# Splitting the gated rows of a hybrid transformer block: ScalarE rounds, VectorE subtracts, GpSimd leaves the chain

## The reference, cut to what matters

```
normed = _rmsnorm(x, scale2)
ffn = _silu(normed @ w_gate.T) * (normed @ w_up.T) @ w_down.T      # 256 -> 1024 -> 256
x = x + ffn
```

## Time and profile before

| | value |
|---|---|
| median of 3 runs | 1556.13 us (1555.75 to 1557.9) |
| the profiled execution | 1559.04 us, of which the profile's span is 1557.0 us |
| TensorE matmul busy | 1467.0 us, 94% of the span |
| VectorE busy | 1104.2 us, 71% |
| ScalarE busy | 664.3 us, 43% |
| GpSimd busy | 556.1 us, 36% |
| turn of the loop | 92.06 us (the same instruction of ScalarE starts at 1005.88 and at 1097.94 us) |

### The profile page before, as it was taken

How to read it: one execution, slowest core, us unless ns; L and a number is a source line. 1 busy time by engine, 2 the same in 40 slices (tenths; PEclk the granted TensorE clock), 3 DMA queues, 4 the chain that set the end, 5 groups by cost and what they waited for, 6 DMA issues and landing times.

```text
span 1557.0 us, 25479 instructions
## 1 busy us (share of the span) xinstructions
PE 1467.0 (94%) x8792; PEld 1047.6 (67%) x8840; DVE 1104.2 (71%) x2127; ACT 664.3 (43%) x971; POOL 556.1 (36%) x705
## 2 busy tenths in 40 slices
PE   8899999999997699999989899999999999999998
PEld 7444444444342478888868687878888787888787
DVE  6888888888888755555585877776867777775542
ACT  1577777777766232223334233323334333332211
POOL 6446555555450232123222322323332232331420
PEclk9899999999998799999999999999999999999999
DMA  4423323323230400101100001001010100100001
GB/s 117 110 57 76 71 56 70 74 62 67 60 73 2 139 28 28 41 28 50 41 14 28 14 1 41 1 15 27 0 40 0 28 13 1 40 0 14 14 1 27
DMA packets 56414, 61.04 MB, mean 39 GB/s; under 512 B 15733, under 2 KB 41637, under 8 KB 56349
## 3 DMA queue, kind: packets, MB, share of 16 engines
q1 hardware_dynamic: 42653, 43.89, 10.7%
q0 software_dynamic: 13408, 16.29, 4.9%
q10 hardware_dynamic: 288, 0.00, 0.0%
HBM read 25.51 MB, written 8.90 MB: 22 GB/s over the span
## 4 chain that ended last, share of the span: by engine, by line
PE 50%; issue 20%; DVE 14%; POOL 8%; ACT 4%; SPq 1%; DMA 1%; another core or an unknown queue 0%; POOLq 0%; DVEq 0%; ACTq 0%
PE ps L1963 14%; PE ps L1991 9%; PE ps L960 5%; PE ps L945 4%; PE ps L931 4%; PE ps L888 3%; POOL h L1566 3%; POOL kT L1539 2%; PE ps L1974 2%; DVE mc L632 2%; PE ps L1949 1%; PE ps L2003 1%; PE ps L898 1%; DVE race L731 1%; DVE top L730 1%
## 5 line engine op out<-in xcount | busy, mean ns | idle before, releaser
L632 DVE TENSOR_REDUCE mc<-ps 128x2 f32<-128x1024 f32 x256 | 305.4, 1220 | 47.3 <-PE ps L931 46.7
L1991 PE MATMUL ps<-w_hi,h 128*128 128x256 f32 x1024 | 220.0, 299 | 11.2 <-DVE h L1803 11.2
L1870 ACT ACTIVATE h<-ps 128x512 fp32r<-128x512 f32 x128 | 76.1, 598 | 315.1 <-PE ps L2021 198.8
L1991 PEld LDWEIGHTS ps<-w_hi,h 128*128 128x128 f32 x1024 | 166.7, 190 | 19.7 <-DVE h L1803 17.6
L346 POOL DMA_DIRECT2D k_st<-k_hi x256 | 124.2, 490 | 141.8 <-PE ps L945 75.7
L1803 DVE SCALAR_TENSOR_TENSOR h<-ps,h 128x512 fp32r<-128x512 f32 x128 | 87.8, 690 | 121.9 <-ACT h L1870 119.2
L1566 POOL TENSOR_TENSOR h<-hf,h 128x512 fp32r<-128x512 f32 x56 | 72.3, 1292 | 277.6 <-DVE h L1816 277.6
L1963 PE MATMUL ps<-xT_b,w_hi 128*128 128x512 f32 x512 | 167.5, 408 | 0.0
L1991 PE MATMUL ps<-w_lo,h 128*128 128x256 f32 x512 | 143.7, 281 | 0.0
L945 PE MATMUL ps<-q_st,k_st 64*128 64x512 f32 x512 | 122.6, 478 | 16.2 <-ACT pT1a L818 5.1
L945 PEld LDWEIGHTS ps<-q_st,k_st 64*128 64x128 f32 x512 | 48.5, 187 | 118.3 <-ACT pT1b L818 46.0
(11 more groups left out here) (276 smaller groups left out, 3439.4 us busy)
## 6 DMA issues: line engine op xcount, KB each, us to landing
q_st<-q_hi SPq DMA_DIRECT2D x256, 32.0 KB, 2.1
k_st<-k_hi POOLq DMA_DIRECT2D x256, 32.0 KB, 1.9
q_st<-q_lo SPq DMA_DIRECT2D x128, 32.0 KB, 2.0
k_st<-k_lo POOLq DMA_DIRECT2D x128, 32.0 KB, 1.9
x<-in_x_dram SPq DMA_DIRECT2D x8, 512.0 KB, 4.0
x_dram<-x SPq DMA_DIRECT2D x8, 512.0 KB, 2.9
yn<-x_dram SPq DMA_DIRECT2D x16, 256.0 KB, 3.7
x<-x_dram SPq DMA_DIRECT2D x16, 256.0 KB, 3.8
```

What stands on the lines that cost most here:

```text
L632: v.tensor_reduce(mc[par][:, qt, 2 * HU + j:MC:NPAIR], ps[:, at:at + 2, :], AX_X, ALU.max).then_inc(max_done, 1)
L1870: a.activation(h[s][m % 2][0][:, :], ps[:, RING[s] + m % 2, :], ACT.Relu).then_inc(F[s]["relu"], 1)
L1991: last = t_.matmul(ps[:, ACC[s] + t // 2, (t % 2) * D:(t % 2 + 1) * D], h[s][m % 2][a][:, t * P:(t + 1) * P], ws[k][:, m, :], start=m == 0 ...
```

## The change

The high part is now written by ScalarE (a Copy activation from `hf`), and the low part by VectorE, as the second half of its step `u`; it waits for ScalarE between its two instructions. GpSimd's function `low_h` is gone. ScalarE's `u` step is new: it waits for the product (`pd`) and, from m = 2 on, for the matmuls that read the buffer (`dm`). All three lists are written anew with the same names in another order. The core of it:

```diff
 def gated(j, m, s=1, S=G):                      # VectorE
     buf = hf[s][m % 2][:, :]
     v.tensor_tensor(buf, ps[:, RING[s] + 1, :], buf, ALU.mult).then_inc(S["pd"], 1)
-    if m >= 2:
-        eng.wait_ge(S["dm"], NM * j + m - 1)
-    elif s == 0:
-        eng.wait_ge(LS["xy"], 1)
-    eng.wait_ge(S["pd"], NM * j + m + 1)
-    v.tensor_copy(h[s][m % 2][0][:, :], buf).then_inc(S["hh"], 1)
+    eng.wait_ge(S["hh"], NM * j + m + 1)
+    hi, lo = h[s][m % 2]
+    v.tensor_tensor(lo[:, :], buf, hi[:, :].bitcast(F32), ALU.subtract).then_inc(S["hl"], 1)
-def low_h(i, s, m, S, done):                    # GpSimd
-    eng.wait_ge(S[done], NM * i + m + 1)
-    hi, lo = h[s][m % 2]
-    g.tensor_tensor(lo[:, :], hf[s][m % 2][:, :], hi[:, :].bitcast(F32), ALU.subtract).then_inc(S["hl"], 1)
+def gated_hi(j, m, s=1, S=G):                   # ScalarE, new
+    if m >= 2:
+        eng.wait_ge(S["dm"], NM * j + m - 1)
+    elif s == 0:
+        eng.wait_ge(LS["xy"], 1)
+    eng.wait_ge(S["pd"], NM * j + m + 1)
+    a.activation(h[s][m % 2][0][:, :], hf[s][m % 2][:, :], ACT.Copy).then_inc(S["hh"], 1)
```

The stretches of the lists that the prediction speaks of, before (-) and after (+):

```diff
 # START, where g first meets rec
-"g.T", "z.o5", "g.m0", "g.u0", "z.o6", "g.m1", "o.x", "g.u1", "z.o7", "z.o8", "g.d0", "g.m2", "rec0", "rec1", "g.u2",
-"rec2", "g.d1", "rec3", "rec4", "g.m3", "rec5", "rec6", "g.u3", "g.d2", "rec7", "z.y", "g.m4", "g.u4", "o.mean"
+"z.o5", "z.o6", "g.T", "z.o7", "z.o8", "g.m0", "rec0", "g.u0", "g.m1", "o.x", "rec1", "g.u1", "rec2", "g.d0", "g.m2",
+"rec3", "g.u2", "g.d1", "rec4", "g.m3", "g.u3", "g.d2", "rec5", "g.m4", "rec6", "g.u4", "g.d3", "rec7", "g.m5", "z.y",
+"g.u5", "o.mean"
 # MERGED, f1 with rec
-"rec5", "f1.m4", "rec6", "f1.d3", "o.rms", "f1.m5", "f1.d4", "f1.m6", "f1.d5", "f1.m7", "f1.d6", "f1.d7"
+"f1.m4", "f1.d3", "rec5", "f1.m5", "f1.d4", "rec6", "f1.m6", "o.rms", "f1.d5", "f1.m7", "f1.d6", "f1.d7"
 # MERGED, g
-"g.m6", "g.u6", "z.rms", "g.d5", "g.m7", "g.u7", "g.d6", "z.T", "g.d7"   # o.wo ahead of g.m6
+"g.m6", "o.wo", "g.u6", "z.rms", "g.d5", "g.m7", "g.u7", "z.T", "g.d6", "g.d7"
 # CLOSE
-"g.u3", ..., "g.m6", "g.u6", "o.T", "g.d5", "z.y", "g.m7", "o.wo", "o.x", "e.rms", "g.u7", "g.d6", "e.gT"
+"o.T", "z.y", "g.u3", "g.d2", "g.m4", "g.u4", "g.d3", "o.wo", "g.m5", "g.u5", "g.d4", "g.m6", "g.u6", "g.d5", "g.m7",
+"o.x", "e.rms", "g.u7", "e.gT"
 # CLOSE, the last names
-"f1.d6", "f0.d6", "f1.d7", "f0.d7", "f1.end", "e.end"
+"f1.d6", "f1.d7", "f1.end", "f0.d6", "f0.d7", "e.end"
```

More of the change, by code:

```diff
@@ L1153 @@
 W_STREAM.insert(W_STREAM.index("g.u1") + 1, "o.x")
-START = ["p0.mask", "p1.mask", "p0.T", "p1.T", "p0.wo", "p1.wo", "init0", "p0.x", "f0.ln", "f0.T", "f0.rt",
[31 rows of a table removed]
+START = ["p0.mask", "p1.mask", "p0.T", "p1.T", "init0", "p0.wo", "p1.wo", "p0.x", "f0.ln", "f0.T", "f0.rt",
[31 rows of a table added]
 def counted(names):
@@ L1198 @@
 BEFORE = list(counted(START))
-MERGED = ["g.T", "rec7", "g.m0", "g.u0", "o.x", "g.m1", "g.u1", "g.d0", "g.m2", "g.u2", "o.mean", "z.y", "o.ln",
[6 rows of a table removed]
-CLOSE = ["g.T", "rec7", "g.m0", "g.u0", "g.m1", "g.u1", "o.mean", "o.ln", "g.d0", "g.m2", "g.u2", "g.d1",
-         "g.m3", "g.u3", "g.d2", "g.m4", "g.u4", "g.d3", "g.m5", "g.u5", "g.d4", "g.m6", "g.u6", "o.T", "g.d5",
-         "z.y", "g.m7", "o.wo", "o.x", "e.rms", "g.u7", "g.d6", "e.gT", "e.x", "g.d7", "g.end", "e.m0", "e.u0",
[7 rows of a table removed]
+MERGED = ["g.T", "rec7", "g.m0", "g.u0", "o.x", "g.m1", "g.u1", "g.d0", "g.m2", "g.u2", "o.mean", "g.d1", "z.y",
[6 rows of a table added]
+CLOSE = ["g.T", "rec7", "g.m0", "g.u0", "g.m1", "g.u1", "o.mean", "g.d0", "o.ln", "g.m2", "g.u2", "g.d1",
[9 rows of a table added]
 Z_NEXT = Z_START[1:] + steps("z.o", NOUT) + ["og"] + steps("rec", T8)[:CUT]
@@ L1579, in pool @@
         parts["e.ln"] = lambda i: ffn_ln(FIRST, 0, last_turn(1))
-        for m in range(NM):
-            parts[f"e.u{m}"] = lambda j, m=m: low_h(0, 0, m, LS, "hh")
-        for m in range(NM):
-            parts[f"g.u{m}"] = lambda j, m=m: low_h(j, 1, m, G, "hh")
         run(eng, parts)
@@ L1936, in act @@
             parts[f"e.m{m}"] = lambda j, m=m: silu(0, m, 0, LS)
+            parts[f"g.u{m}"] = lambda j, m=m: gated_hi(j, m)
+            parts[f"e.u{m}"] = lambda j, m=m: gated_hi(0, m, 0, LS)
         parts |= {"e.gT": lambda j: high(last_turn(0), 0, s2), "e.T": lambda j: high(last_turn(1), 0)}
```

## The result

The changed kernel takes 1548.99 us, the median of 5 runs (1547.52 to 1550.66). The kernel before took 1556.28 us beside it (5 runs, 1555.75 to 1557.9). The ratio is 0.9946 with a 95% interval of 0.9936 to 0.9957: 0.5% faster, 7 to 8 us. Forecast was 1547, with 1543 to 1551 as its own range. The profiled execution took 1549.59 us (span 1547.8), 0.6 us above this median; that of before took 1559.04, 2.8 us above its own. So the two traces lie 9.2 us apart where the medians lie 7.3 apart.

What follows compares the result with a forecast made beforehand. TensorE was taken to bound the kernel, busy 1467.0 of 1557.0 us. Terms of -5.1 (closing), -3.0 (loop), 0, 0 and -0.8 (end) summed to -8.9, put on the 1556.13 median: 1547 us, range 1543 to 1551.

Steps and rivals of the forecast that it cites:

- The closing stretch: After the loop: two TensorE waits and the slow clock go (5.8 us), a later Silu costs 0.7; -5.1 us.
- the loop: Five turns, each 0.6 us shorter from the dense and routed parts together; -3.0 us in all.
- `START`: Opening list: routed steps and weight splits only shuffled with the same contents; 0 us, bounds -3 and +3.
- the tail: Kernel's end: the last `f1` block's store starts two `d` earlier and doesn't share the DMA queue; -0.8 us.
- the late Silu: Tile 3's Silu comes about 0.9 us later behind ScalarE's rounding, stalling TensorE's next gate by 0.7 us.
- The routed part of a turn: In the loop: the 0.71 us wait shrinks to 0.1, the 0.48 stays, 0.3 of small gaps go.
- The dense part of a turn: In the loop: new stalls of 0.7 and 0.3 us against gains of 0.45 and 0.2; 0.3 us slower.
- rival C: VectorE's new subtraction is held by GpSimd's `o.x` or decay steps, costing TensorE 5 us; 1552 us, chance 0.08.
- rival A: Only the closing stretch and the end gain; in the loop new stalls eat the routed part's gain; 1550 us, chance 0.20.
- Where `g` meets `rec`: First meeting, 860 to 900 us: old stalls and slow clock (9 us) replaced by equal new stalls; 0, bounds -6 and +5.
- B: VectorE becomes the bound of the dense part, each turn paying 2 us; slower, 1564 us, chance 0.15.
- D: The first meeting also loses its stalls and slow clock without new ones, -6 us more; 1541 us, chance 0.12.

Runs made afterwards that it cites:

- e3: The changed kernel with the CLOSE list of the kernel before: 1557.91 us, ratio 1.0004.
- e4: The kernel before in its old roles, with the new CLOSE list but `o.x` moved behind `rec7`: 1553.58 us, ratio 0.9978.
- e6: The changed kernel with one GpSimd wait more, so that in the loop `o.x` starts after the low part of tile 1: 1546.28 us, ratio 0.9924.
- e1: The changed kernel's new roles with all three lists of the kernel before: 1563.61 us, ratio 1.0042.
- e2: The kernel before in its old roles, with only the START list of the changed kernel: 1561.42 us, ratio 1.0033.
- e10: The roles of e9 (ScalarE rounds, GpSimd subtracts) with the lists of e8: 1555.39 us, ratio 0.9985.
- e8: The kernel before in its old roles, with the new early START, the new routed part of MERGED and the CLOSE of e4: 1548.26 us, ratio 0.9936.
- e9: e1 with the subtraction given back to GpSimd, ScalarE still rounding, lists of the kernel before: 1564.53 us, ratio 1.0043.
- e5: The changed kernel with the Silu `g.m3` moved ahead of `o.ln`, and `z.y` behind it, in MERGED: 1550.77 us, ratio 0.9949.
- e11: The changed kernel with the later `o.x` of e6 and `g.d5` moved behind `g.u7` in MERGED: 1546.12 us, ratio 0.9919.

## Why the prediction was right, and where it was not

The time was right to 2 us, the direction too. The closing stretch, on which most of the sum rested, went as reasoned. That the rest fits too is partly luck: the loop gave 2.5 us less than its term, and `START`, put at nothing, gave about as much. By its steps:

**The closing stretch: right.** Predicted -5.1, measured -5.2 from the first gate to the last matmul. For the tail predicted -0.8, measured -0.6: the four transfers took 3.3 us to land, 3.8 in the earlier trace rows. GpSimd in the closing stretch of after: the addition near its head, then nothing for 21.69 us, until ScalarE's squares call for the root:
```profile
1414.82 2.40 POOL L1555 TENSOR_TENSOR x<-x,y 128x1024 f32<-128x1024 f32 x1 [15.09 <-DMA out_dram<-x]
...
1438.91 1.02 POOL L1475 TENSOR_TENSOR squares<-squares,plus_half 128x4 f32<-128x4 f32 x1 [21.69 <-ACT pr L1907]
```
TensorE's only wait between 1385 and 1460 us is the one for the late Silu, 0.7 predicted:
```profile
1424.82 0.73 PE L1960 MATMUL ps<-xT_b,w_gate_b_hi 128*128 128x512 f32 x2 [0.51 <-ACT hf L1879]
```
The waits of 2.09 and 1.04 us and the slow clock behind them are gone. e3 shows that it is this list, e4 that most of it (4.4 of 5.85 us with the tail) needs no new roles.

**The routed part of a turn: right.** From the mask to the first gate, 32.85 us became 32.10 (-0.75; -0.9 predicted). TensorE's waits for its low part, are 4.1 us instead of 7.4:
```profile
PE ps L1988 <- DVE h L1793: 4.1, 6, 0.7
PE ps L1960 <- ACT hf L1879: 3.5, 6, 0.6
```
The one that stays is 0.70 us long.

**The dense part of a turn: the mechanism right, two sizes wrong.** From the first gate to the keys' projection, 39.98 us became 40.69 (+0.71; +0.3 predicted). The Silu comes late as described. In one turn of after, the Silu and the gate that waits for it, to be set beside the earlier trace rows:
```profile
1060.80 0.60 ACT L1879 ACTIVATE hf<-ps 128x512 f32<-128x512 f32 x1
...
1061.45 0.73 PE L1960 MATMUL ps<-xT_b,w_gate_b_hi 128*128 128x512 f32 x2 [0.59 <-ACT hf L1879]
```
It costs 0.85 us (the `d` group 2.15 instead of 1.40, the gate after it 1.50 instead of 1.40) where I had 0.7. The wait at `d7` went as predicted; its group and the transposes give 0.70, but `d6` and `d7` now take 3.19 us instead of 2.91, so the gain is 0.42 net, where I had 0.45 less 0.3. The 0.2 us that the shorter chain should give at `d0` and `d1` became a loss of 0.24: the up product before `d0` takes 1.70 us instead of 1.46, because the subtraction of tile 0 took 1.39 us beside `o.x` (e6). That was rival C's mechanism, in the place where I argued against it: `o.x` did run beside the multiplication (1047.09, 0.69 us long, undisturbed), but at 2.41 us it is long enough to reach the subtraction too.

The Trainium skill, SBUF — State Buffer, "Who interferes with whom", says that a VectorE instruction with two SBUF inputs contends with a GpSimd instruction that reads SBUF, and that the port pair they share is an exclusive lock. By that the second would wait fully. Here the subtraction began at 1048.48 and the addition ended at 1049.32; waiting that 0.84 us and then running 0.69 would make 1.53, and 1.39 was measured. The trace agrees within 0.14 us. By the same section a VectorE instruction with one SBUF input at most, outside the modes that use both port pairs, is free of this; the multiplication, whose other input is in PSUM, agrees with its 0.69 us.

**The loop: mis-sized.** The term was -3.0 us and measured -0.5. A turn should have given 0.6 and gave nothing, because +0.71 and -0.75 cancel. Most of the error is in the dense part, 0.4 us a turn worse than its term; the routed part is 0.15 short of its own. This is what rival A said of the loop.

**The routed steps of START: the step that failed.** "In `START` the routed steps and weight splits are shuffled with the same contents: 0" was worth -2.7 us between the two traces, of which 1.2 to 2.4 stand against all kernels with the old order. The windows of before and after, for this stretch alone (same columns as the earlier trace rows):
```profile
544.00:734.00 190.00, 185.13 (x1220) 160.15 (x1237) 104.91 (x313) 49.63 (x85) 54.87 (x44) 0.99 0.10 31
```
```profile
544.00:732.00 188.00, 185.21 (x1224) 159.84 (x1242) 103.29 (x309) 48.83 (x85) 53.41 (x46) 1.00 0.11 32
```
The same work in 2 us less. TensorE's waits in the whole stretch sum to 4.3 us before, 3.6 in e1 and e4 with the same order, and 2.2 after: the waits for the rows of the transposes (1.7 us before) are gone, and this is the list's. The trace of before also lost clock at 660 to 670 us. That is not the list's, for e1, with the same order, ran there at full clock. Before and then e1:
```profile
660.00:670.00 10.00, 9.61 (x59) 8.57 (x59) 5.40 (x26) 2.52 (x4) 4.75 (x2) 0.84 0.00 0
```
```profile
660.00:670.00 10.00, 9.68 (x68) 8.22 (x66) 6.66 (x28) 3.10 (x5) 4.58 (x2) 1.00 0.00 0
```
I had looked at the stretches with the new instructions only; the bounds of 3 us held it. e2 gives the same stage with none of the new instructions.

**Where `g` meets `rec`: right, by compensation.** Predicted 0, measured +0.6. The waits are others, as said; the timeline of after, for the earlier trace rows:
```profile
842.27 0.74 PE L1960 MATMUL ps<-xT_b,w_gate_b_hi 128*128 128x512 f32 x2 [1.37 <-DVE xT_b L1647]
...
877.35 1.09 PE L2066 MATMUL ps<-ident,oT_b 128*128 128x128 f32 x8 [2.62 <-DVE oT_b L1740]
```
The wait at `o.mean` is 2.6 us where I found 3.2, the one after `g.T` 1.4 for 1.7. The clock is 0.96 instead of 0.91.

**The rivals.** B is out: VectorE never became the bound, a turn stayed at 92.0. A was right of the loop; its total, 1550, is no farther from the 1549 measured than the forecast of 1547, and it too had nothing for START. C's mechanism is real at 0.3 to 0.44 us a turn, some 2 us in all, not the 5 us priced. D didn't come.

What stays open: of e10 against e8 (7 us) the turns hold 5.7; the next 2.8 us stand where `g` meets `rec`, in a stage that varies by more than 1 us from profile to profile. That ScalarE's rounding ahead of the squares is what delays the Silu is read from the order and the timelines of e1 and e9; no kernel was run with the rounding behind the squares.

## What to carry to other kernels

Before crediting a change of engines, run its new order with the old engines: here the order alone gave 0.6%, order and engines together 0.5%. When a resource leaves a chain, ask what still runs on it beside the new instructions, for its whole length, and not only at its start. And a list that is "only shuffled" has a value of its own: read its waits as carefully as those of the part that is edited. And when a stage's gain comes from two traces, look for other kernels that run the same stage: here 1.2 of 2.7 us was chance.

## What the runs showed of the hardware

- A wait can cost TensorE more than its length, and neither its length nor the code tells whether it will. In e2 the wait of 4.58 us was followed by sums of 3.35 us that take 1.77 in after. The windows of e2 there show a granted clock of 0.50, the lower of the two levels, and then 0.78:
```profile
873.00:877.00 4.00, 3.73 (x6) 2.00 (x7) 3.75 (x5) 0.00 (x0) 2.08 (x1) 0.50 0.01 2
877.00:881.00 4.00, 4.00 (x20) 3.23 (x19) 3.83 (x5) 0.00 (x0) 0.00 (x0) 0.78 0.00 0
```
In after the wait of 2.62 us at 877.35 passed at full clock:
```profile
874.00:880.00 6.00, 3.38 (x26) 2.85 (x25) 5.21 (x7) 2.92 (x5) 0.00 (x0) 1.00 0.33 90
```
e5 has the same order at this place and the same wait (2.60 us), 0.01 us later in its trace, and there the clock fell; the transposes behind it took 1.97 us instead of 1.09:
```profile
874.00:880.00 6.00, 3.40 (x17) 2.92 (x16) 5.17 (x7) 2.68 (x5) 0.00 (x0) 0.73 0.36 90
```
- The clock also fell without such a wait: in before it was 0.50 from 668 to 670 us, and in the ten us ahead of that the timeline shows one wait of TensorE, 0.32 us at 663.73. In e1 and e4, with the same order, it did not fall there.
- The attention ahead of the first mask is the same code in all kernels; its length varied by 3.1 us between profiles (542.2 to 545.3), more than the step from e6 to e11. Differences of this size are to be read per stage.
